# Two groups of heads in one bank of sums: the attentions of a two-lane decoder kernel, with the lanes' order made anew

## What is computed

```python
q = (Q @ WQ_w.T + WQ_b).reshape(b, s, H, D_K).transpose(0, 2, 1, 3)
k, v = ...                                   # the same from K and V
scores = jnp.einsum('bhqd,bhkd->bhqk', q, k) / jnp.sqrt(D_K)
scores = jnp.where(mask == 0, 1e-09, scores) # cross; causal: jnp.where(causal, att, -inf)
attn = jax.nn.softmax(scores, axis=-1)
out = jnp.einsum('bhqk,bhkd->bhqd', attn, v)
out = out.transpose(0, 2, 1, 3).reshape(b, s, D_MODEL)
return out @ WO_w.T + WO_b
```

## Time and profile before

| | us |
|---|---|
| median of 3 runs | 1412.91 |
| lowest and highest | 1410.71, 1414.18 |
| the profiled execution | 1408.09 |
| its span, first to last instruction | 1406.4 |

### The profile page before, as it was taken

How to read it: one execution, slowest core, us unless ns; L and a number is a source line. 1 busy time by engine, 2 the same in 40 slices (tenths; PEclk the granted TensorE clock), 3 DMA queues, 4 the chain that set the end, 5 groups by cost and what they waited for, 6 DMA issues and landing times.

```text
span 1406.4 us, 20670 instructions
## 1 busy us (share of the span) xinstructions
PE 1182.3 (84%) x7705; PEld 693.5 (49%) x7766; DVE 758.4 (54%) x1977; ACT 672.0 (48%) x1164; POOL 344.1 (24%) x735
## 2 busy tenths in 40 slices
PE   7849767888789999969987877778869999978986
PEld 5735421344344667734565441244434467754455
DVE  2834586574594321278345577557487331159343
ACT  1115369724238643316743538934317753324751
POOL 3121120341235200034403121043324400032510
PEclk8778667877699999999999968878679999999988
DMA  7031000120330000060014100021150000042011
GB/s 240 2 77 41 10 0 1 51 56 7 99 91 3 5 1 1 1 180 3 3 61 106 28 10 1 2 64 43 48 141 3 4 2 1 0 131 51 3 38 38
DMA packets 48354, 57.92 MB, mean 41 GB/s; under 512 B 16469, under 2 KB 41349, under 8 KB 47750
## 3 DMA queue, kind: packets, MB, share of 16 engines
q1 hardware_dynamic: 47390, 56.11, 15.0%
q10 hardware_dynamic: 864, 0.48, 0.1%
HBM read 35.11 MB, written 20.87 MB: 40 GB/s over the span
## 4 chain that ended last, share of the span: by engine, by line
PE 62%; DVE 17%; ACT 9%; POOL 4%; DMA 3%; issue 3%; SPq 1%; another core or an unknown queue 0%; ACTq 0%; POOLq 0%; DVEq 0%
PE banks L1607 10%; PE banks L1597 9%; ACT sb_arena L1291 5%; PE banks L1414 5%; PE banks L1402 4%; PE banks L597 4%; PE banks L1389 3%; PE banks L468 3%; DVE sb_rmax L1542 3%; PE banks L949 2%; PE banks L463 2%; DMA sb_qs<-sb_mrows 2%; DVE sb_arena L1337 1%; DVE sb_st L440 1%; PE banks L913 1%
## 5 line engine op out<-in xcount | busy, mean ns | idle before, releaser
L1542 DVE TENSOR_REDUCE sb_rmax<-banks 128x1 f32<-128x512 f32 (+3 forms) x352 | 204.4, 635 | 67.0 <-PE banks L1391 66.4
L1471 ACT ACTIVATE sb_arena<-banks 128x512 f32<-128x512 f32 x320 | 175.2, 598 | 99.3 <-PE banks L1402 90.1
L1291 ACT ACTIVATE sb_arena<-banks,sb_zk 128x512 f32<-128x512 f32 x256 | 153.1, 800 | 9.3 <-PE banks L1241 9.3
L458 POOL TENSOR_SCALAR sb_var<-sb_mv 128x4 f32<-128x4 f32 x40 | 13.3, 333 | 587.3 <-DVE sb_mv L443 587.3
L1662 ACT ACTIVATE sb_arena<-banks,sb_b 128x512 f32<-128x512 f32 x128 | 87.5, 687 | 132.8 <-PE banks L1597 131.5
L1500 POOL TENSOR_SCALAR_AFFINE_SELECT sb_arena<-sb_arena 128x256 f32<-128x256 f32 x256 | 99.0, 409 | 177.6 <-ACT sb_arena L1471 177.2
L1389 PE MATMUL banks<-sb_arena,sb_qs 128*128 128x256 bf16 (+3 forms) x492 | 119.6, 313 | 26.5 <-DVE sb_rmax L1542 19.9
L1607 PEld LDWEIGHTS banks<-sb_w,sb_arena 128*128 128x128 f32 x1024 | 124.9, 192 | 30.5 <-issue 29.7
L1721 DVE SCALAR_TENSOR_TENSOR sb_xall<-banks,sb_region,sb_xall 128x128 f32<-128x128 f32 x160 | 44.9, 344 | 162.6 <-PE banks L1607 162.6
L1607 PE MATMUL banks<-sb_w,sb_arena 128*128 128x128 f32 x1024 | 126.2, 275 | 0.0
L1597 PE MATMUL banks<-sb_ft,sb_w 128*128 128x512 f32 x256 | 123.7, 597 | 0.6 <-ACT sb_arena L1662 0.6
(11 more groups left out here) (281 smaller groups left out, 1936.6 us busy)
## 6 DMA issues: line engine op xcount, KB each, us to landing
sb_qs<-q_scratch SPq DMA_DIRECT2D x32, 288.0 KB, 4.7
q_scratch<-sb_region SPq DMA_DIRECT2D x16, 384.0 KB, 2.6
sb_arena<-k_scratch SPq DMA_DIRECT2D x16, 288.0 KB, 6.8
sb_arena<-in_chosen SPq DMA_DIRECT2D x8, 514.0 KB, 4.1
sb_w<-in_w SPq DMA_DIRECT2D x2, 2048.0 KB
q_scratch<-sb_region SPq DMA_DIRECT2D x16, 256.0 KB, 2.2
sb_qs<-q_scratch SPq DMA_DIRECT2D x32, 96.0 KB, 2.4
k_scratch<-sb_region SPq DMA_DIRECT2D x8, 384.0 KB, 2.6
```

The costliest lines, as they stand in the source:

```text
L1291: i = nc.scalar.activation(L.dist[h % 3][:, kb, :], (b2_, b3)[h % 2], ACT.Abs, bias=L.zk[:, kb, h:h + 1])
L1471: nc.scalar.activation(L.probs[:, u % SLOTS, :], bank_of(SELF_ORDER, ring, ("key", u)), ACT.Exp)\
L1542: nc.vector.tensor_reduce(L.rmax[:, t, g * GROUP + h0:g * GROUP + h0 + nh], bank_of(SELF_ORDER, ring, ("max", step))[:, 0:nh * kl] .rearra ...
```

## The change

The values move one head to the right in their buffer: head h lies at column `(h + 1) * OW`. An even group takes 32 stationary columns from `h * OW`, so its own nine columns land in rows 9 to 17 of its 32, and what the neighbour left in rows 0 to 8. An odd group takes only its own nine columns and writes rows 0 to 8 over that (`sums_of`), in the same bank, without a wait for a copy. After each odd group one copy takes both groups to `L.osb[:, g // 2, :]`; the wait for it stands ahead of group 2 and in the finish. `gather` has two parts, rows 9 to 17 for the even and 0 to 8 for the odd group, so one matmul of 72 columns gathers eight heads; there are 8 in a stage instead of 16, and the steps of the finish go from 8 to 4 on PE, those of the copies from 4 to 2 on ACT. `COUNTS` of `osb` for BU stays at `G`. The strings of `ORDER` are new for all five engines; only SP's is printed here, the others are left out.

```diff
--- before.py
+++ after.py
@@ -28,11 +28,13 @@
 REL = 16
 
 
+
 GROUP = 4
 G = H // GROUP
+PAIRS = G // 2
 VW = 32
 OW = HD + 1
-VALUES = H * OW + VW - OW
+VALUES = OW + H * OW + VW - 2 * OW
 
 
 
@@ -138,7 +140,7 @@
 _ATT = {"turned": 2, "q": 1, "q32": 1, "q_split": 3, "q_parked": PARKED, "cleared": EDGES,
         "q_first": STACKED, "q_rest": STACKED,
         "k": 1, "k32": 1, "k_split": 3, "k_parked": PARKED, "k_first": STACKED, "v": 1, "values": 1,
-        "negmax": G, "mparts": G, "mturned": G, "mrows": G, "osb": G, "spread": 2, "att": 2, "ft": 2, "y": 1, "res": 1}
+        "negmax": G, "mparts": G, "mturned": G, "mrows": G, "osb": PAIRS, "spread": 2, "att": 2, "ft": 2, "y": 1, "res": 1}
 _CROSS = {**_ATT, **_LN, "masks": 1, "mask_loaded": 32, "tok": G * T, "maxed": G * T, "key": H, "probs": H, "pv": G}
 _SELF = {**_ATT, **_LN, "xb": 1, "k_rest": STACKED, "mstacked": 16 * G, "tok": G * NM, "maxed": G * NM, "key": G * NK, "probs": G * NK,
          "cut": G * NK // 2, "pv": G * len(SETS)}
@@ -167,28 +169,28 @@
 ORDER = {
     "SP":
-    "3055d943e00ff901fe69a03f9598019fd0fe007fe01fe53a03f95998",
+    "2fa516bc1ff006fe01ac5fc06a67fe422f01ff801fe01ac5fc06a648",
...
@@ -356,7 +358,7 @@
         zkbias = sb("zkbias", [128, H])
         zqbias = sb("zqbias", [H, 1])
         fold = sb("fold", [128, VW])
-        gather = sb("gather", [128, GROUP, OW])
+        gather = sb("gather", [128, 2, GROUP, OW])
         relcol = sb("relcol", [128, 7])
         ident = sb("ident", [128, 128])
         identb = sb("identb", [128, 128], BF16)
@@ -528,7 +530,13 @@
 
         def values_of(buffer, h):
 
-            return buffer[:, h * OW:h * OW + VW]
+
+            return buffer[:, (h + 1) * OW:(h + 2) * OW] if h // GROUP % 2 else buffer[:, h * OW:h * OW + VW]
+
+        def sums_of(acc, h):
+
+            at = h % GROUP * VW
+            return acc[at:at + OW] if h // GROUP % 2 else acc[at:at + VW]
 
         def split_max(pool, L, p, g):
 
@@ -587,15 +595,15 @@
 
             yield
             for pair in range(2):
-                for g in range(G):
-                    if pair or g:
+                for two in range(PAIRS):
+                    if pair or two:
                         yield
-                    pe.wait_ge(*p.at("osb", g + 1))
+                    pe.wait_ge(*p.at("osb", two + 1))
                     for n in range(2):
                         t = 2 * pair + n
-                        at = (n * G + g) * GROUP * OW
-                        i = nc.tensor.matmul(ring[pair][:, at:at + GROUP * OW], L.osb[:, g, t * 128:(t + 1) * 128],
-                                             gather[:].rearrange("p j c -> p (j c)"), start=True, stop=True)
+                        at = (n * G + 2 * two) * GROUP * OW
+                        i = nc.tensor.matmul(ring[pair][:, at:at + 2 * GROUP * OW], L.osb[:, two, t * 128:(t + 1) * 128],
+                                             gather[:].rearrange("p r j c -> p (r j c)"), start=True, stop=True)
                 i.then_inc(L.sem("spread"), 1)
             yield
             for t in range(T):
@@ -942,11 +950,11 @@
 
             def weighted_values(g):
                 pe.wait_ge(*p.at("probs", GROUP * (g + 1)))
-                if g:
-                    pe.wait_ge(*p.at("osb", g))
+                if g and g % 2 == 0:
+                    pe.wait_ge(*p.at("osb", g // 2))
                 for i in range(GROUP):
                     h = g * GROUP + i
-                    last = nc.tensor.matmul(acc[VW * i:VW * (i + 1), :], values_of(L.cvalues, h), L.probs[0:K2, h % SLOTS, :],
+                    last = nc.tensor.matmul(sums_of(acc, h), values_of(L.cvalues, h), L.probs[0:K2, h % SLOTS, :],
                                             start=True, stop=True)
                 last.then_inc(L.sem("pv"), 1)
 
@@ -1025,10 +1033,10 @@
                     nc.scalar.activation(L.probs[0:K2, h % SLOTS, :], bank_of(order, ring, ("key", h))[0:K2, :], ACT.Exp)\
                         .then_inc(L.sem("probs"), 1)
                 g = cross_out(step, j)
-                if g is not None:
+                if g is not None and g % 2:
                     yield
                     act.wait_ge(*p.at("pv", g + 1))
-                    nc.scalar.activation(L.osb[:, g, :], acc, ACT.Copy).then_inc(L.sem("osb"), 1)
+                    nc.scalar.activation(L.osb[:, g // 2, :], acc, ACT.Copy).then_inc(L.sem("osb"), 1)
             yield from finish_scalar(act, L, p, ring)
 
         def cross_pool(pool, L, p):
@@ -1072,7 +1080,7 @@
             order = CROSS_ORDER[j]
             yield
             dve.wait_ge(*p.at("v", 1))
-            dst = L.cvalues[:, 0:H * OW].rearrange("p (h c) -> p h c", c=OW)[:, :, 0:HD]
+            dst = L.cvalues[:, OW:(H + 1) * OW].rearrange("p (h c) -> p h c", c=OW)[:, :, 0:HD]
             src = b3[0:K2, 0:128].rearrange("p (h d) -> p h d", d=HD)
             if j:
                 nc.vector.tensor_tensor(dst, src, rows[0:K2, R["x1_v"], :].rearrange("p (h d) -> p h d", d=HD), ALU.add)\
@@ -1406,12 +1414,13 @@
             def weighted_values(g, v):
                 tiles, n_units = SETS[v]
                 pe.wait_ge(*p.at("cut", (NK * g + n_units) // 2))
-                if g and v == 0:
-                    pe.wait_ge(*p.at("osb", g))
+                if g and g % 2 == 0 and v == 0:
+                    pe.wait_ge(*p.at("osb", g // 2))
                 for kb in tiles:
                     for j in range(GROUP):
                         n, at = next((n, at) for n, unit in enumerate(KEY_UNITS) for i, k, at in unit if (i, k) == (j, kb))
-                        last = nc.tensor.matmul(acc[VW * j:VW * (j + 1), kb * 128:S], values_of(L.values[:, kb, :], g * GROUP + j),
+                        last = nc.tensor.matmul(sums_of(acc, j + g * GROUP)[:, kb * 128:S],
+                                                values_of(L.values[:, kb, :], g * GROUP + j),
                                                 L.probs[:, (NK * g + n) % SLOTS, at:at + S - kb * 128],
                                                 start=(kb == 0), stop=(kb == 2))
                 last.then_inc(L.sem("pv"), 1)
@@ -1523,7 +1532,7 @@
             yield from split_vector(dve, L, p, "q", L.qpart, L.nrm[:].rearrange("p t n -> p (t n)"), L.q32[:])
             yield
             dve.wait_ge(*p.at("v", 1))
-            dst = L.values[:, :, 0:H * OW].rearrange("p t (h c) -> p t h c", c=OW)[:, :, :, 0:HD]
+            dst = L.values[:, :, OW:(H + 1) * OW].rearrange("p t (h c) -> p t h c", c=OW)[:, :, :, 0:HD]
             nc.vector.tensor_tensor(dst, tok(ring[2]).rearrange("p t (h d) -> p t h d", d=HD),
                                     rows[:, R[f"s{l}_v"], :].rearrange("p (h d) -> p h d", d=HD).unsqueeze(1)
                                     .to_broadcast([128, T, H, HD]), ALU.add).then_inc(L.sem("values"), 1)
@@ -1858,9 +1867,10 @@
         sel[part * 32:part * 32 + H] = np.eye(H)
         for j in range(GROUP):
             msel[j % 2 * 3 * GROUP // 2 + part * GROUP // 2 + j // 2, j] = 1
-    gather = np.zeros((128, GROUP, OW), np.float32)
-    for j in range(GROUP):
-        gather[j * VW:j * VW + OW, j] = np.eye(OW)
+    gather = np.zeros((128, 2, GROUP, OW), np.float32)
+    for r in range(2):
+        for j in range(GROUP):
+            gather[j * VW + (1 - r) * OW:j * VW + (2 - r) * OW, r, j] = np.eye(OW)
 
     def all_parts(a, n):
         return np.broadcast_to(np.concatenate(a).reshape(1, n), (128, n))
```

34 lines of the change are left out of this document (17 added, 17 removed).

## The result

The kernel after takes 1361.45 us (median of 4 runs, 1355.18 to 1369.50) against 1413.55 us (median of 4 runs) for the kernel before on the same chip: ratio 0.9626, 95% interval 0.9562 to 0.9691. Its profiled execution took 1363.61 us. Executions come in two states; ratios and mean clocks in this text take only those in the faster one, medians take all. Two later measurements of the same kernel on other chips gave 0.9565 (0.9527 to 0.9603) and 0.9598 (0.9544 to 0.9652). So it is about 4% faster, some 52 to 65 us, where the prediction said 1.8% and a range whose lower end is 1368 us. The direction was right, the size was not: about 27 us were missed, and the experiments are about them.

What follows compares the result with a forecast made beforehand. It took the matrix engine to set the end in most stretches, not all. Terms -27.3 - 3 + 2 + 1 + 3 = -24.3 us took the profiled 1408.1 to 1383.8; with 4.8 up to the median, 1388 us, range 1368 to 1406.

Steps and rivals of the forecast that it cites:

- Gathering matmuls, -27.3: Attention finishes: half of the gathering passes' 57.7 us on the chain goes, less 1.6 us; bounds -29 and -25.5.
- +2: Each finish: fewer passes cover the last copy, opening up to 0.35 us, 5.6 us in all; +2 us taken.
- +1: Each finish: fewer passes of pair 1 cover VectorE's division of pair 0, at most 0.1 us each; +1 us.
- +3: Finishes: a tenth of the gain given back, since other work, such as maxima or exponentials, stands next in line; +3 us.
- the 1.6 that stood for wide passes: Gathering: 72-column passes cost 0.02 us more each in five of 16 finishes taken as run at a lowered clock.
- Copies, -3: Copies of the sums, 64 to 32: the matrix engine's 6.5 us of waits shrink; -3 us, bounds 0 and -6.5.
- The order, 0 +- 12: New instruction order: much the same plan mirrored, worth 0, bound 12 us, 5% of 224 us idle time.
- The prediction's own test: One sign of being wrong: a stage of 100 us without any attention changes its length.
- Weighted values, 0: Weighted-value matmuls with 9 stationary columns in odd groups: column tiles still run side by side; 0 us, bound -4.
- rival (c): Weighted values: the 9-column tiles no longer run side by side, 138 us slower, 1526 us; chance 0.03.
- rival (e): Gathering: passes cost by their width, 0.22 instead of 0.113 us, so no effect, 1415 us; chance 0.05.
- Rival (b): Whole kernel: the new order is the larger part, taking 22 us more of idle time, 1366 us; chance 0.08.

Runs made afterwards that it cites:

- half_narrow: Kernel before with only the odd groups gathered, by 8 matmuls of 36 columns a finish, even groups left out: 1388.82 us, ratio 0.9782.
- half_gather_2: Kernel before with only the odd groups gathered, by 8 matmuls of 72 columns a finish, second measurement: 1378.90 us, ratio 0.9708.
- wide_gather: Kernel before with all 16 gathering matmuls kept, each moving 108 columns in place of 36: 1397.44 us, ratio 0.9843.
- half_copy: Kernel before without the copies of groups 0 and 2 and the waits for them, all 16 gathering matmuls kept: 1408.34 us, ratio 0.9895.
- half_wait: Kernel before without the waits of groups 1 and 3; copies of a constant replace those of groups 0 and 2: 1414.73 us, ratio 0.9886.
- half_wide: Kernel before with only the odd groups gathered, by 8 matmuls of 108 columns a finish: 1384.25 us, ratio 0.9744.

## Why the prediction was wrong

It said -24.3 us; measured are -52 us in the first comparison and -57 as the mean of three (0.9596). No single step holds the 33 us between: against the mean, the order was off by 13, the copies by 9 to 12, the clock by 8 to 12 and the halving by 8, and these overlap by 5 to 12 us. By its own steps:

**Gathering matmuls, -27.3, with +2, +1 and +3 given back (right in kind, too small by some 8).** All that was said of the pass holds: 0.12 us at 72 columns and full clock, 256 records, the share of the chain from 4.1% to 2%. Removal at unchanged width gave 31 us (half_narrow). For that kernel the sum has 22.9: the 27.3, the 1.6 that stood for wide passes, less the 6 given back, since its finish is as short as the changed one. No run shows the 3 us for "something stands next in line". The finish behind VectorE's routing does still wait, as the earlier trace rows had it: in the kernel after the second transposition at 689.63 us waits 1.33 us for the division, but that is one of the two where it was expected. The chain's 57.7 us held the finishes at a lowered clock at their full length, so the halving of these was counted; seven of the 16 ran at a mean clock below 0.9, not five.

**The clock, no term (a step that failed).** The text had the numbers in its hand: finishes at 0.60 and 0.51 while the matrix engine was busy 5.99 of 6.1 us. The prediction used them to charge wide passes up to 0.04 us more, and never asked what would become of the clock itself if the passes moved twice the columns. Its sign was wrong as well: 1.6 us of surcharge stand where the wide passes bring 6 to 10 us at equal count (half_gather_2 against half_narrow), and 22 us where all 16 are kept (wide_gather). The mean granted clock of 0.859 goes to 0.862, 0.875 and 0.888 in the three.

The Trainium skill, "TensorE: Matmul & The Clock Gate", section "HAM oscillation — how this bites in real kernels", puts a clock that falls back in mid-kernel down to gaps in which TensorE idles. The traces here don't bear this out as the whole cause: about the first finish half_narrow waits 0.87, 0.23 and 0.45 us and half_gather_2 0.87, 0.20 and 0.46, and the clock falls only in the first. By that rule alone half_gather_2 and wide_gather would have changed nothing.

**Copies, -3, bounds 0 and -6.5 (mis-sized).** 12 to 15 us (half_copy; half_wait 8 to 16), about 8 us at a held clock. The bound was taken from the row of the matrix engine's waits for the copy, 6.5 us. That row counts only idle time of which the copy was the last cause. A wait that goes can also let what is queued behind it start earlier, where the waiting was put down to other causes. half_copy's idle time is 1410.4 - 1193.1 = 217 us against 224 (both profiles lack 61 matmul records), and the wait rows themselves fell to

```profile
PE banks L949 <- ACT sb_region L1032: 0.8, 2, 0.4
PE banks L1415 <- ACT sb_region L1479: 0.4, 1, 0.4
```

(us, times, longest). These two rows explain 5.3 of the 12 to 15 us. The one profiled execution has a span above that of before, so the rest is seen in the runs alone, and by which later waits it came is not shown. That ScalarE's freed 15 us are worth nothing agrees with the ratio of half_wait; its median leaves room for a few microseconds.

**The order, 0 +- 12 (value wrong, bound a little small).** About 13 us, 8 to 19. The count of step positions said that the plan was much the same, mirrored. It isn't: the same changed kernel works 8.2 us more in 65 with it, long before the first shortened finish. The prediction's own test, a stage without any of these attentions that changes its length, came out against it: from 87.7 to 82.1 us in the first (79.6 and 79.5 in two more profiles of the kernel after), and from 87.0 to 95.4 in the distance-kernel stage. The plan does the same on the kernel before (89.0 to 79.0), where it gives nothing in all. Two plans with nearly equal shares of stage pairs can fill waits quite differently, and for this the strings give no price.

**Weighted values, 0.** Right, by the 9- and 32-column rows above; rival (c), 1526 us, and rival (e), 1415 us, are ruled out by these rows and the pass of 0.12 us.

**The range.** Rival (b), the order as the larger part, gave 1366 us and was nearest, but for a reason that holds a fourth of the truth. With one term each for width, waits and order missing or small, and all on the same side, the argument "they will not all fall on one side" failed: terms that act on one and the same idle time and one clock are not independent.

**How it adds up.** Halving at equal width 31, width 6 to 10, copies 12 to 15, order 13: 62 to 69 us for parts that together give 57. Without the order, 49 to 56 for a whole of 44 (0.9687). So the parts overlap by 5 to 12 us; to which of them the overlap belongs these runs don't show. Open too is why the wide and halved kernel (half_wide) loses the clock of 0.888 again.

## What to carry to other kernels

Before pricing an edit to TensorE's passes, look up the granted clock where they run; if it is lowered though the engine is busy, ask what the edit does to the clock, and try the same work with more columns in each pass: on the kernel before that brought 1.6% with no work removed. A row of waits was no upper bound of what the wait costs: 6.5 us in the rows, of which 5.3 went, against 12 to 15 in the runs. Compare the idle times of two profiles only where as many records are missing in both: 61 matmul records made some 10 us here. When an edit comes with a new order, run the edit with the old order: the order was worth 13 us of 57 here, and nothing on the kernel without the edit.

## What the hardware showed that was not expected

Stretches of 32 fp32 passes with 36 moved columns and a weight load of 128 each ran at a granted clock of 0.60 and 0.51 in the kernel before, the lower of the two levels (1.2 GHz) for most of the time. The first of them ran at 1.00 (2.4 GHz) in half_copy, but the clock fell 0.6 us behind its end. In the four profiles with 36 columns on that plan the clock fell 1.2 to 4.4 us after the first finish began, in the five with 72 or 108 after 18.0 to 27.2, with gaps of the same length about it in half_narrow and half_gather_2. Up to 108 columns such a pass costs next to nothing more at full clock: 32 fill 3.62 us with 36 columns and 3.76 with 108; at 144 it does, 2.39 us for 16 against 2.11 at 72. And a mean clock higher by 0.012 between two versions of the changed kernel (0.878 and 0.890) brought no more than 4 us, while 0.029 between the kernel before and its wide version brought 22. Our reading, which no run tests, is that a raised clock is worth something only where the matrix engine sets the end.
